# Causal stage: which of three PSUM slots an item takes, by estimated release in place of strict turn

## The reference, cut to what matters

```python
x = x + _L0_attn_ref(_layernorm(x), ...)   # windowed attention, window 64, 16 heads of 8
x = x + _L0_ffn_ref(_layernorm(x), ...)    # gated linear attention, 8 heads of 64, 4 routes
x = x + _L1_attn_ref(_layernorm(x), ...)   # causal softmax attention, and a linear recurrence
x = x + _L1_ffn_ref(_layernorm(x), ...)    # mixture of 16 experts, top 2, and a shared expert
```

```python
scores = jnp.einsum('bhid,bhjd->bhij', q, k) * scale        # 4 x 16 heads, 1024 x 1024
attn = jax.nn.softmax(scores + causal_mask, axis=-1)
y_softmax = jnp.einsum('bhij,bhjd->bhid', attn, v)
state = retention * state + Gamma * hebbian                  # scan over the 1024 tokens
y = alpha * y_softmax + (1.0 - alpha) * y_stp
return y @ out_w + out_b
```

## Time and profile before

| what | value |
|---|---|
| median of 3 runs | 1822.01 us (1821.84 to 1822.9) |
| the profiled execution | 1816.52 us |
| its span in the profile | 1815.2 us |
| causal stage, first `M` to last `W` | 945 to 1560 us of the span |

### The profile page before, as it was taken

One profiled execution on the slowest core, in us unless ns is written; L12 is line 12 of the kernel. 1 busy time (PEld: TensorE's weight loads), 2 busy tenths in 40 slices (PEclk: granted clock), 3 DMA queues, 4 the chain that ended last, 5 costly groups with the idle time before them and its releaser, 6 DMA issues. The chain is left out here.

```text
span 1815.2 us, 45480 instructions
## 1 busy us (share of the span) xinstructions
PE 1583.7 (87%) x19664; PEld 1003.4 (55%) x19664; DVE 1273.6 (70%) x2035; ACT 1109.5 (61%) x1650; POOL 696.6 (38%) x500
## 2 busy tenths in 40 slices
PE   4688988999999999999976878888888888899999
PEld 2455656778777778777853323433433332566665
DVE  4665745777677667766768768768778886766564
ACT  3265676777777777777733567667577678433321
POOL 4212302444444345424531545556465554301100
PEclk8798998999999999999996989999999999999999
DMA  7863200000000000000142472164236223000000
GB/s 182 216 153 109 41 16 1 2 2 2 1 2 2 2 2 2 2 2 2 48 105 64 126 176 72 49 181 100 66 109 154 71 65 79 1 7 12 7 12 13
DMA packets 43357, 102.30 MB, mean 56 GB/s; under 512 B 3944, under 2 KB 12288, under 8 KB 41428
## 3 DMA queue, kind: packets, MB, share of 16 engines
q1 hardware_dynamic: 40244, 93.88, 19.9%
q10 hardware_dynamic: 2912, 5.51, 1.7%
HBM read 67.12 MB, written 31.46 MB: 54 GB/s over the span
## 5 line engine op out<-in xcount | busy, mean ns | idle before, releaser
L1450 DVE TENSOR_REDUCE arena<-ring 128x2 f32<-128x1024 f32 (+2 forms) x320 | 341.8, 1109 | 89.3 <-PE ring L1307 62.4
L1550 ACT ACTIVATE arena<-ring 128x1024 f32<-128x1024 f32 (+1 forms) x320 | 291.3, 937 | 129.8 <-PE ring L1336 90.6
L1357 PE MATMUL accs<-arena 128*9 128x512 f32 (+3 forms) x1536 | 174.4, 528 | 2.7 <-ACT arena L1550 2.6
L2511 POOL TENSOR_TENSOR arena<-arena 128x1280 f32<-128x1280 f32 x28 | 65.3, 2333 | 283.2 <-PE accs L2272 245.9
L1300 PE MATMUL ring<-arena 48*128 48x512 bf16 (+3 forms) x768 | 126.4, 341 | 44.3 <-DVE arena L1450 23.6
L1329 PE MATMUL ring<-arena 51*128 51x512 bf16 (+3 forms) x768 | 123.8, 340 | 45.4 <-DVE arena L1450 25.9
L2503 POOL TENSOR_TENSOR arena<-arena 128x512 f32<-128x512 f32 x112 | 141.3, 1294 | 3.0 <-DVE arena L2313 3.0
L292 POOL TENSOR_SCALAR xn<-x,moments,rstd 128x128 f32<-128x128 f32 x80 | 64.5, 823 | 198.7 <-DVE rstd L263 183.3
L2778 ACT ACTIVATE arena<-ring 128x512 f32<-128x512 f32 x80 | 47.8, 597 | 147.3 <-PE ring L2633 140.5
L2496 POOL TENSOR_TENSOR arena<-arena 128x1024 f32<-128x1024 f32 x32 | 84.6, 2644 | 122.7 <-DVE arena L2370 122.7
L2738 DVE TENSOR_TENSOR arena<-arena,ring 128x512 f32<-128x512 f32 x80 | 55.0, 687 | 87.9 <-PE ring L2635 74.5
(11 more groups left out here) (346 smaller groups left out, 4239.3 us busy)
## 6 DMA issues: line engine op xcount, KB each, us to landing
arena<-whole_k SPq DMA_DIRECT2D x32, 512.0 KB, 4.7
arena<-whole_q SPq DMA_DIRECT2D x32, 512.0 KB, 6.4
arena<-c_scratch_q SPq DMA_DIRECT2D x14, 384.0 KB, 8.7
arena<-c_scratch_k SPq DMA_DIRECT2D x14, 384.0 KB, 11.8
a_scratch_k<-arena SPq DMA_DIRECT2D x8, 512.0 KB, 4.0
c_scratch_k<-arena SPq DMA_DIRECT2D x8, 512.0 KB, 3.7
arena<-a_scratch_q SPq DMA_DIRECT2D x9, 384.0 KB, 7.0
arena<-a_scratch_k SPq DMA_DIRECT2D x9, 384.0 KB, 9.0
```

Source lines behind the costliest of these rows:

```text
L1357: mm = nc.tensor.matmul(acc[ci % 2][32 * h:32 * h + HD + 1, a - c * BANK:BANK], c_values[b % 2][:, j, r * HEADS // 2 + 2 * g + i, :], weig ...
L1450: nc.vector.tensor_reduce(dst, src, AX.X, ALU.max, negate=True).then_inc(c_max_taken.up(item), 1)
L1550: nc.scalar.activation(view(c_probs[wi % 4]), view(ps), ACT.Exp).then_inc(c_weights_made.up(item), 1)
```

## The change

The planner keeps `free` by slot instead of by age. An item on the ring takes the slot with the smallest estimated release (`free.index(min(free))`), and the planner gives out, beside the order, the slot of every item (`place_of`). `causal` uses these places; items for which the planner has no estimate (those after its loop) take the slot that was used longest ago. PE waits for the item that held the same slot before (`held_before`) in place of the one three back. `begin` uses `min(free)`, so the planner's clocks, and with them the order, can come out different too. The matmuls, the readers and the three slots stay as they are.

```diff
             free, made = [0.0, 0.0, 0.0], {}
-            order = []
+            order, place_of = [], {}
...
                 if times(item)[2]:
-                    t = max(t, free[0])
+                    t = max(t, min(free))
...
                 if on_ring:
-                    free.append(done + HOP)
-                    free.pop(0)
+                    place_of[item] = free.index(min(free))
+                    free[place_of[item]] = done + HOP
...
-            slot = {}
+            slot, held_before, last_used = {}, {}, [(0, None), (1, None), (2, None)]
             for item in order:
                 if item[0] in on_ring or item[0] == "next" and item[1] in MOE_ON_RING:
-                    slot[item] = ring[len(slot) % 3]
+                    k = place_of[item] if item in place_of else last_used.index(min(last_used))
+                    slot[item], held_before[item] = ring[k], last_used[k][1]
+                    last_used[k] = len(slot) + 2, item
...
-                    if ps is not None:
-                        if len(taken) >= 3:
-                            pe_wait_free(taken[-3])
-                        taken.append(item)
+                    if held_before.get(item):
+                        pe_wait_free(held_before[item])
```

More of the change, by code:

```diff
@@ L1192, in causal_order @@
             assert not end
-            return order
+            return order, place_of
         def causal():
             s = "c"
-            order = causal_order()
+            order, place_of = causal_order()
             on_ring = ("turn", "q", "k", "gate1", "gate2", "beta", "vT", "v", "M", "S", "W", "att", "tp")
-            slot = {}
+            slot, held_before, last_used = {}, {}, [(0, None), (1, None), (2, None)]
             for item in order:
                 if item[0] in on_ring or item[0] == "next" and item[1] in MOE_ON_RING:
-                    slot[item] = ring[len(slot) % 3]
+                    k = place_of[item] if item in place_of else last_used.index(min(last_used))
+                    slot[item], held_before[item] = ring[k], last_used[k][1]
+                    last_used[k] = len(slot) + 2, item
             w_items = [i for i in order if i[0] == "W"]
@@ L1242, in pe_program @@
             def pe_program():
-                taken = []
                 pe.wait_ge(weights_in[s], "all")
```

## The result

The changed kernel takes 1826.55 us (median of 20 runs, 1818.78 to 1835.66), the kernel before 1821.92 us (20 runs). The ratio is 1.003, with a 95% interval of 1.0016 to 1.0045. The forecast was 1819.0 us and no measurable change; the time lies in the range of 1810 to 1829, but outside the likeliest case's own 1818.4 to 1825.6, on the side of the rival "slower". Two single executions of later runs, at 2566.5 and 5348.19 us, are left out of all figures.

What follows compares the result with a forecast made beforehand. Bound: waits between engines coupled by the ring in the causal stage. Losses 4.25 less wins 9.8 gave -5.6 us, about half carried on: -3, all else zero, so 1822.0 to 1819.0 us; range 1810 to 1829.

Steps and rivals of the forecast that it cites:

- the likeliest case: No measurable change over the whole kernel: wins and losses offset each other, -3 us, 1818.4 to 1825.6 us; chance 0.42.
- the rival "slower": Ring slots released later than estimated are named on purpose; +4.3 us, with one more stall about +7, 1829 us; chance 0.22.
- What bounds the kernel: Causal stage: no engine full, PE's idle 118.5 us are waits between engines coupled by the ring; fourth layer: nothing to gain.
- Wins: Causal stage: 27 takes where the newly named slot was really free earlier, 13.65 us in sum, 9.8 us once capped.
- its cap: Each win counts only up to PE's work before the next take; at 1049.89 us, 0.61 of 4.18 us.
- Losses: Causal stage: 20 takes where estimates name the wrong slot, 9.18 us in sum, 4.25 us after slack.
- this slack: A later PE start costs nothing while the item's reader still has other work; lowers the losses to 4.25 us.
- All else equal: Each of the 53 differing takes was valued by its own win or loss on the timeline of before.
- A new order: Shifted planner clocks change the order of M, V and W somewhere; taken as zero, 7 us either way.
- such slow stretches are a small part: Causal stage: with a granted clock of 0.93, stretches of slowed matmuls after idle PE were held to be few.
- The Trainium skill's rule: Recurring gaps on PE mean too few buffers; with still three slots, naming them otherwise regains nothing, sum 0.

Runs made afterwards that it cites:

- the wins alone: Kernel before, old order; the oldest slot passed over only at takes its trace showed to win; 0.9984 to the kernel before, 2.9 us less.
- the losses: Kernel before, old order; the oldest slot passed over only at the 20 takes its trace showed to lose; 1.0044, 8.0 us more.
- all new slots: Kernel before with its old order kept and every slot chosen by smallest estimated release; 1.0051 to the kernel before, 9.3 us more.
- the run with `gate1` put right: Old order, slots by estimated release, with the slot of gate1 entered as free 2.5 us earlier; 1.0038 to the kernel before.
- the late takes alone: Old order, strict turn in the first 132 takes, slots by estimated release in the 592 after them; 1.0045 to the kernel before.
- the early ones: Old order, slots by estimated release in the first 132 takes, strict turn after them; 1.003 to the kernel before.
- The doubled matmuls: Score matmuls of each M done twice in the first two units: 1.0023 with estimated slots in the first 132 takes, 1.0022 in the kernel before.
- The measured slots: Slots named by hand from traces, strict turn elsewhere: old order (47 takes) 0.9968, repeated 0.999; changed kernel's order (37 takes) 0.9967, to the kernel before.

## Why the prediction was wrong

*What bounds the kernel* held: the fourth layer kept its 255 us, and the two profiles differ by 6 us in the causal stage, where the medians differ by 4.6.

*Wins.* At 1049.9 the forecast held to 0.1 us, with its cap. I let half of 9.8 us carry on, 4.9; the wins alone (25 takes) measured 2.9 us, with an interval that reaches from 6.7 less to 0.9 more. The size is not refuted.

*Losses: the step that failed.* "Taking this slack off each loss leaves 4.25 us", of which half was to carry on, so 2.1. Alone they measured 8.0 us (5.3 to 10.7), near the 9.18 that stood there as the whole. So this term of the sum was too small by a factor of nearly four, and that turned -3 us into a loss. Why is shown only in part. The slack of one item's reader covers that item, but PE works its list in order, and I had named that queue ("the whole of PE's list") and then priced only the item in front. In the traces this leaves 0.3 us at each of three `tp` takes, and nothing at the three largest takes, where the items behind catch up. The other part goes with the clock: beside the kernel before, that of the losses is lower by 0.0047, which at the slope given below is 4.5 of the 9.2 us between the means of the runs. Whether and how the losing takes bring it down stays open. The rival "slower" had its point of decision at losses whole against halved wins, +4.3 us; measured +4.6. The agreement owes something to luck, since the parts that it adds up are others (8.0 and 2.9 in place of 9.18 and 4.9, a sum of 5.1 where all new slots measured 9.3).

*All else equal: a second failure, of coverage.* The picks were valued one by one in the state of strict turn. Once an over-estimated slot has been passed over, it is passed over again: on the old order 57 takes left the turn where I had counted 53, four of my wins gone and eight others new. Wins and losses alone add up to +5.1 us, all new slots together measured +9.3. The intervals of the three allow these 4 us to be chance, and what part the eight have wasn't shown; the run with `gate1` put right moved the right way, but less than its interval.

*A new order: zero*, was right in its price, 1.0001, though `M`, `W` and `V` stand otherwise in 414 of 832 places (320 `M`, 320 `W`, and 192 `V`, which are 12 a unit and not 16). Part of this is luck: the zero was the middle of plus and minus 7 us, with no reason for it.

*The clock: a term I set to zero.* "So such slow stretches are a small part" was wrong for this size of effect. Within the runs of one kernel, the time follows the granted clock: over 309 runs of all kernels here, with a level for each, 9.6 us less for each 0.01 more (5.4 to 16.8 in single kernels). The changed kernel, in its 12 runs beside 33 of before, has a clock lower by 0.0054 (0.9457 against 0.9511), which at that slope is 5.2 us of the 5.9 between the two means. For the late takes alone it is 3.7 of 8.8 us, for the early ones 6.7 of 6.4. This is a correlation, and its direction isn't shown: PE's matmuls took 0.61 us after its idle 4.98 us, so a kernel with more waits may have the lower clock from them. The doubled matmuls agree with a causal reading for the early takes, but leave the rival named there. What in the slots makes the mean clock fall stays open.

*The Trainium skill's rule* (Perfetto Trace Analysis, Optimization Strategy: recurring gaps can mean too few buffers) gave a sum of 0. No run here had a fourth slot, so it isn't tested. The measured slots, at ratios of 0.9968, 0.999 and 0.9967 with three slots, make it likely that the choice of slot is worth something too.

## What to carry to other kernels

- When a wait on an in-order queue moves, follow every item behind it, by the reader of each, until the shift is gone or stays. Slack of the waiting item's own reader is only part of the answer. Here the shift was gone 11 us on at the three largest takes, and stayed at three `tp` takes, 0.3 us each.
- Naming a buffer by estimate is only as good as the estimate's order of releases, and strict turn has a virtue that estimates lack: it can't leave a free slot unused for long. Here the names by estimate lost 0.3%, where names from a trace won 0.3% in two runs of three. Take the names from a trace, and test them.
- Compare the granted clock over many runs beside the time, and count it as a term of the sum of its own: of PE's time, not of its waits. A single pair of profiles exaggerates it: the two here have 0.956 and 0.940 over their spans, the means of the runs are 0.952 and 0.945.

## What the hardware showed beyond that

Runs of one program differ by 17 us (1818.78 to 1835.66), with clocks of 0.951 in the fastest and 0.943 in the slowest. PE's matmuls at the lower level take nearly twice as long (eight `V` matmuls 1.90 us against 1.05), in an engine that is idle 20% of the stage, and half of that still reaches the end: 0.01 of 1820 us is 18 us of lost full-speed time, and the slope is 9.6 us. With extra, useless matmuls the kernel with the new early slots had a mean clock of 0.9543 (0.0021 over the kernel before beside it), and without them 0.9459 (0.0070 under it). Its time gained nothing that can be told: 1.0023 with them and 1.003 without.
